# Moving the routing of the seventh batch into the last two groups of attention, and packing the eighth batch's steps closer

## The chip, the cores and the metric
The kernel runs on one core of a Trainium2 chip. The metric is the device time in microseconds (us) of the whole program. The engines are PE (TensorE, matrix products), DVE (VectorE), ACT (ScalarE), POOL (GpSimd) and SP (SyncE, which here only issues DMAs). Each engine works through its own list of instructions in order; semaphores tie the lists together, and an engine that waits holds back everything behind the wait in its own list.

## The reference
One transformer block with adaptive layer norm, 8 batches of 512 tokens, width 128, in float32:

```python
mod = (_silu(L0_c) @ L0_wmod).reshape(L0_c.shape[0], 6, 1, -1)
sa, ca, ga, sb, cb, gb = (mod[:, 0], mod[:, 1], mod[:, 2], mod[:, 3], mod[:, 4], mod[:, 5])
ga = (2 * (ga >= 0) - 1) * jnp.maximum(jnp.abs(ga), 0.25)
gb = (2 * (gb >= 0) - 1) * jnp.maximum(jnp.abs(gb), 0.25)
h = _layernorm(x, axis=-1) * (1 + ca) + sa
x = x + ga * _L0_attn_ref(h, L0_attn_Wq, L0_attn_Wk, L0_attn_Wv)
h = _layernorm(x, axis=-1) * (1 + cb) + sb
x = x + gb * _L0_ffn_ref(h, L0_ffn_router_w, L0_ffn_w1, L0_ffn_b1, L0_ffn_w2, L0_ffn_b2)
return x
```

The attention has 16 query heads of 8 and one shared key and value head. The feed-forward part is a mixture of 8 experts (128 to 512 to 128, exact GELU): a router gives each token 8 logits, the two largest are kept, and their experts' outputs are mixed by the softmax of the two logits.

## The kernel before, in words
The program has three stages. The first (`prepare_*`) normalises the input and computes queries, keys and values. The second is attention in 32 groups (`GROUPS`) of four heads: batch b has the groups 4b to 4b+3. The third is the expert stage: tokens have been scattered into rows sorted by expert (`h_sorted` in DRAM), and 78 tiles (`NTILES`) of 128 rows are worked through, 55 for the batches 0 to 5 (`TILES[0]`) and 23 for the batches 6 and 7. Batches are counted from 0, so the seventh is batch 6 (`LAST - 1`) and the eighth batch 7 (`LAST`).

**A group of attention.** For each of four blocks s of 128 keys, PE makes the scores of four heads in two halves u (`scores`, L957), ACT exponentiates each half (`exponentials`, L1134) and PE multiplies by the values (`values`, L967). Two groups ahead, PE makes the scores once more for the maxima (`maximum`, L926), which DVE takes (`take_maximum`, L1275); ACT copies the turned maxima (L1159), POOL splits them (`split`, L72 to L75) and SP moves them into the operands (`shift`, L819). So in the groups 30 and 31 there are no maxima left to take, and DVE has little to do. After a group, ACT copies its result out (`out_of_bank`, L1127) and SP moves the rows of its heads together by five DMAs (`regroup`, L829 and L830).

**Steps of a batch after its attention.** They are written into the loops by hand, a fixed number of groups after the batch: sums and heads are turned (PE L932 and L982, ACT copies L1150 and L1169), the attention is divided, gated and added (`add_attention`, L618, L620, L622), statistics (`stats`, L1291, on DVE), variance (L631 to L639), reciprocal root (`newton_root`, L647 to L652, always on POOL), normalised rows (`normalize_rows`, L1144, on ACT), `rows` (L661 to L665), rows turned (`turn_batch`, PE L1001, ACT copy L1173), router logits (PE L1009, ACT L1177), `top_two` (L688 to L700), `ranks` (PE L1018 and L1019, ACT L1183), `slots` (L720 to L727), and `route` (L734): two indirect DMAs of 128 rows each, for each of four blocks of tokens, so eight DMAs a batch, issued by POOL. For the batches 0 to 5 all of this lies in attention. For batch 6 the last part of it, and for batch 7 all of it, stands in the loop over tiles at fixed tile numbers (`if t == 8: turn_batch(LAST - 1)`), on each engine's list for itself.

**A tile t of the expert stage.** SP loads its rows (`load_tile`, L853). PE turns tile t+4 (`turn_rows`, L1026), makes the first product of tile t+2 (`up`, L1035) and the second of tile t (`down`, L1046). ACT applies GELU in four instructions (`gelu`, L1190). DVE copies the turned tile (`transposed`, L1307), its destination rows (L1311) and the expert's weights (`weights`, L1300), and adds the second bias (`results`, L1319). POOL scatters the result (`scatter`, L1469, one indirect DMA per tile). ACT runs up to two tiles ahead of DVE's `results`.

**Between the chunks.** When batches 0 to 5 are placed, DVE numbers the tiles (`count_tiles`, `number_tiles`), and SP writes filling rows behind each expert's rows (`fill`, L837, eight DMAs in two halves around the last `regroup`s). The same comes again for the batches 6 and 7: `fill(1, ...)` stands in SP's list between the loads of tile 54 and tile 55, and tile 55 can be loaded only when batches 6 and 7 are routed and filled.

**Order at the end of attention.** SP issues the loads of the tiles 0 to 7, then `regroup` of group 31 (L829 and L830, at `t == XD - 1`), then the load of tile 8. PE sets out on tile 0 when attention, weights and tile numbers are there.

## Time and profile before
| | |
|---|---|
| median of three runs | 681.05 us (680.46 to 684.31) |
| profiled execution | 677.33 us, of which the span from first to last instruction is 675.5 us |
| PE busy | 595.8 us (88%) |
| DVE busy | 497.0 us (74%) |
| ACT busy | 448.8 us (66%) |
| POOL busy | 356.6 us (53%) |
| DMA | 49.65 MB, mean 74 GB/s |

The durations below come from the one profiled execution, the median from three others. The prepare stage and attention take the first 470 us, the tiles from there to 656 us, and the last loads, mixing and stores the remaining 20 us. Busy shares are averages over stages with different limits, so the rows that count are those of the end of attention and of the expert stage. In a row of a timeline, the square brackets give the idle time of the engine just before it and the line that ended it; "remote" means that the profile found no instruction of an engine that ended it.

### The profile page before, as it was taken

The page shows a single profiled execution, that of the slowest core. Times are in us where ns is not written, and L with a number is a line of the kernel's source. Part 1 is how long each engine was busy: PE and PEld are TensorE (multiplying, and loading weights), DVE is VectorE, ACT ScalarE, POOL GpSimd, SP SyncE. Part 2 cuts the span into 40 slices and gives each one's busy share as a digit, 9 for nine tenths or more (in the row PEclk, how much of TensorE's full clock was granted, in tenths as well). Part 3 has the DMA queues.
Part 4 walks back from the last instruction along what each step waited for, and adds up shares of the span by engine and source line. Part 5 has one row for each costly group of instructions (what it writes and reads, how often), then busy time and mean ns, then how long its engine had stood idle before and what let it go on. Part 6 is the DMA issues. An engine that isn't in the chain of part 4 may idle for free.

```text
span 675.5 us, 19379 instructions
## 1 busy us (share of the span) xinstructions
PE 595.8 (88%) x6826; PEld 329.5 (49%) x6826; DVE 497.0 (74%) x1113; ACT 448.8 (66%) x795; POOL 356.6 (53%) x602
## 2 busy tenths in 40 slices
PE   2897999999999999999999999977997969779980
PEld 1342234433433433433433433422997969769980
DVE  5578999898887787798797797762565645555876
ACT  2473488888878778778778778658654534355771
POOL 5785101143465575675575675655454555645571
PEclk9897999999999999999999999979997998899995
DMA  7763500210300300301301300011221222224634
GB/s 214 272 180 101 148 8 12 75 27 9 93 16 23 102 18 22 102 16 31 95 15 31 95 15 24 20 50 45 70 72 43 68 54 69 64 68 128 200 100 148
DMA packets 46766, 49.65 MB, mean 74 GB/s; under 512 B 11168, under 2 KB 40912, under 8 KB 45936
## 3 DMA queue, kind: packets, MB, share of 16 engines
q1 hardware_dynamic: 38928, 37.20, 20.5%
q0 software_dynamic: 4544, 9.38, 4.2%
q10 hardware_dynamic: 3200, 1.84, 0.9%
q8 instruction: 57, 0.93, 0.6%
q14 instruction: 37, 0.30, 0.2%
HBM read 30.30 MB, written 17.47 MB: 71 GB/s over the span
## 4 chain that ended last, share of the span: by engine, by line
PE 64%; DVE 13%; issue 5%; POOL 5%; ACT 4%; SPq 4%; another core or an unknown queue 2%; DMA 2%; POOLq 0%; DVEq 0%; ACTq 0%
PE ps L926 14%; PE ps L967 14%; PE ps L957 12%; DVE neg_max L1275 11%; PE ps L1046 8%; PE ps L1035 7%; POOL P L258 4%; ACT P L1134 1%; ACT parts L1190 1%; PE ps L994 1%; PE ps L1009 1%; PE ps L945 1%; PE ps L1026 1%; SPq L829 1%
## 5 line engine op out<-in xcount | busy, mean ns | idle before, releaser
L1275 DVE TENSOR_REDUCE neg_max<-ps 128x1 f32<-128x512 f32 x512 | 320.0, 681 | 63.5 <-PE ps L926 55.4
L1134 ACT ACTIVATE P<-ps,zero 128x1024 f32<-128x1024 f32 x256 | 272.5, 1111 | 83.5 <-PE ps L957 79.2
L926 PE MATMUL ps<-K,Q 128*32 128x512 bf16 x2048 | 187.0, 386 | 7.1 <-DVE neg_max L1275 3.1
L957 PE MATMUL ps<-Q,K 128*32 128x512 bf16 x2048 | 156.7, 383 | 10.8 <-ACT P L1134 7.7
L967 PE MATMUL ps<-P,V 128*32 128x512 f32 x1024 | 134.8, 601 | 1.1 <-ACT P L1134 0.8
L1469 POOL DMA_INDIRECT y_rows<-P,to_now x78 | 78.8, 1010 | 83.9 <-DVE to_now L1311 36.4
L926 PEld LDWEIGHTS ps<-K,Q 128*32 128x32 bf16 x2048 | 54.0, 95 | 126.0 <-DVE neg_max L1275 75.8
L1190 ACT ACTIVATE parts<-ps,parts 128x128 f32<-128x128 f32 x252 | 70.5, 378 | 64.3 <-PE ps L1035 25.2
L957 PEld LDWEIGHTS ps<-Q,K 128*32 128x32 bf16 x2048 | 50.9, 97 | 78.8 <-issue 32.1
L1046 PE MATMUL ps<-W,parts 128*128 x504 | 72.2, 289 | 10.6 <-ACT parts L1190 9.6
L734 POOL DMA_INDIRECT h_sorted<-diag,slot x64 | 63.9, 998 | 28.3 <-POOL max_parts L75 13.3
L1035 PE MATMUL ps<-parts 128*128 128x128 f32 x504 | 71.0, 284 | 4.9 <-issue 3.9
L1046 PEld LDWEIGHTS ps<-W,parts 128*128 128x128 f32 x504 | 65.1, 202 | 12.1 <-issue 11.7
L1035 PEld LDWEIGHTS ps<-parts 128*128 128x128 f32 x504 | 64.5, 199 | 7.3 <-issue 5.7
L72 POOL CAST max_parts<-neg_max_T 16x128 bf16<-16x128 f32 x32 | 8.9, 279 | 111.7 <-ACT neg_max_T L1159 111.7
L1300 DVE COPY parts<-W 128x644 f32 x63 | 33.1, 525 | 19.8 <-issue 10.4
L1319 DVE TENSOR_TENSOR P<-ps,parts 128x128 f32<-128x128 f32 x63 | 17.8, 284 | 35.5 <-PE ps L1046 20.7
L967 PEld LDWEIGHTS ps<-P,V 128*32 128x32 f32 x1024 | 30.4, 110 | 20.9 <-issue 2.9
L258 POOL TENSOR_SCALAR P<-X,ln_mean,ln_rstd 128x128 f32<-128x128 f32 x28 | 26.3, 949 | 4.3 <-DVE ln_rstd L390 4.2
L1307 DVE COPY parts<-ps 128x128 f32<-128x128 f32 x63 | 17.8, 283 | 11.6 <-PE ps L1026 10.7
L1190 ACT ACTIVATE P<-ps,P 128x128 f32<-128x128 f32 x60 | 17.2, 380 | 11.0 <-PE ps L1035 6.2
L1026 PE MATMUL ps<-consts,xs 128*128 128x128 f32 x78 | 21.8, 284 | 0.9 <-DMA xs<-h_sorted 0.9
(203 smaller groups left out, 616.5 us busy)
## 6 DMA issues: line engine op xcount, KB each, us to landing
Q<-q_parts SPq DMA_DIRECT2D x24, 384.0 KB
xs<-h_sorted SPq DMA_DIRECT2D x78, 65.0 KB
W<-w_t SPq DMA_DIRECT2D x2, 2048.0 KB, 10.7
q_parts<-parts SPq DMA_DIRECT2D x8, 384.0 KB
Q<-y_rows SPq DMA_DIRECT2D x6, 512.0 KB
diag<-att_u SPq DMA_DIRECT2D x128, 16.0 KB
Q<-max_parts SPq DMA_DIRECT2D x96, 4.0 KB
out<-Q SPq DMA_DIRECT2D x6, 256.0 KB, 2.3
```

The source lines that it names most:

```text
L258: eng.tensor_scalar(xn[b % 2][:, t, :], X[:, n, :], ln_mean[:, n:n + 1], ln_rstd[:, n:n + 1], ALU.subtract, ALU.mult).then_inc(done, 1)
L734: eng.indirect_dma_start(h_sorted[chunk_of(b)], bass.IndirectOffsetOnAxis(ap=slot[p][:, k, t:t + 1], axis=0), hs[p][:, t, :], None).then_i ...
L926: ins = eng.matmul(ring_bank(*unit)[QUAD * q:QUAD * (q + 1), :], Q[buffer_of(g)][:, g % NG * G + j, at:at + QUAD], K[buffer_of(g)][:, 0, : ...
L957: ins = eng.matmul(bank(2 * u + j)[QUAD * q:QUAD * (q + 1), :], K[p][:, 1, at:at + QUAD], Q[p][:, g % NG * G + 2 * u + j, :], start=True, ...
L967: ins = eng.matmul(bank(7)[QUAD * j:QUAD * (j + 1), :], V[buffer_of(g)][:, s, :], P[s % 2][:, j, :], start=(s == 0), stop=(s == T - 1), ti ...
L1035: ins = eng.matmul(bank(t % UD)[:, TS * c:TS * (c + 1)], w1_now[t % HD][:, 128 * c:128 * (c + 1)], xsT[t % HD], start=True, stop=True)
L1046: ins = eng.matmul(bank(DOWN_BANK[t % 2])[:, 0:D], hid[t % HD][:, c, :], W2[:, bass.ds(e, 1), c, :].rearrange("p a d -> p (a d)"), start=( ...
L1134: nc.scalar.activation(P[s % 2][:, 2 * u:2 * u + 2, :], bank(2 * u, 2).rearrange("p (j t) -> p j t", j=2), ACT.Exp, bias=zero[:], scale=SC ...
L1190: nc.scalar.activation(hid[t % HD][:, c, :], bank(t % UD)[:, TS * c:TS * (c + 1)], ACT.Gelu, bias=w1_now[t % HD][:, F + c:F + c + 1]).then ...
L1275: eng.tensor_reduce(neg_max[g % 2][:, j * T + s:j * T + s + 1], ring_bank("maximum", g, s, j), AX.X, ALU.max, negate=True).then_inc(ring_u ...
L1300: eng.tensor_copy(w1_now[t % HD], W1[:, bass.ds(e, 1), :].rearrange("p a d -> p (a d)")).then_inc(w_copied, 1)
L1469: eng.indirect_dma_start(y_rows, bass.IndirectOffsetOnAxis(ap=to_now[t % YD][:], axis=0), ys[t % YD], None).then_inc(scattered[t % YD], 16)
```

## The change
All of batch 6's steps up to its slots leave the loop over tiles. In group 30 DVE adds the attention of batch 6, takes its statistics and variance ahead of `count_tiles` and `number_tiles`, and makes its `rows` after them. POOL's part is the reciprocal root alone, put between two routes of batch 5. ACT normalises the four blocks before the half (3, 0) of group 30. In group 31 PE turns the rows and makes the logits, ACT copies both, DVE ranks them (`top_two`); PE makes the ranks after its last values, ACT copies them before it loads the GELU table, and DVE makes the slots before its first `transposed`. POOL routes batch 6 after the scatters 1, 3, 5 and 7.

`regroup` of group 31 moves from SP's list to ACT's (`regroup_last`), before the first GELU. The steps of batch 7 are set to earlier tiles, in the same order and on the same engines as before; its `normalize_rows` is split over two tiles.

```diff
+        TURN_LATE, LOGITS_LATE = (GROUPS - 1, 0, 3), (GROUPS - 1, 1, 3)
...
                 for t in range(NTILES):
                     load_tile(t)
-                    if t == XD - 1:
-                        regroup(GROUPS - 1)
...
+                            if (g, s, j) == TURN_LATE:
+                                turn_batch(LAST - 1)
+                            if (g, s, j) == LOGITS_LATE:
+                                logits(LAST - 1)
...
                 values(GROUPS - 1, T - 1)
+                ranks(LAST - 1)
                 eng.wait_ge(experts_loaded, START + 4 * 16)
                 eng.wait_ge(ring_used, START + len(USED_AT))
-                eng.wait_ge(ring_copied, START + COPIED_AT["sums turned", LAST])
+                eng.wait_ge(ring_copied, START + COPIED_AT["ranks", LAST - 1])
...
+                    if t == 0:
+                        turn_sums(LAST)
                     if t == 2:
-                        turn_sums(LAST)
-                    if t == 5:
                         turn_heads(LAST)
-                    if t == 8:
-                        turn_batch(LAST - 1)
-                    if t == 11:
-                        logits(LAST - 1)
-                    if t == 19:
-                        ranks(LAST - 1)
-                    if t == 21:
+                    if t == 15:
                         turn_batch(LAST)
-                    if t == 24:
+                    if t == 17:
                         logits(LAST)
-                    if t == 32:
+                    if t == 22:
                         ranks(LAST)
...
+                def regroup_last():
+
+                    g = GROUPS - 1
+                    eng.wait_ge(att_out, START + g + 1)
+                    for j in range(G):
+                        at = ((NG - 1) * G + j) * DK
+                        eng.dma_start(heads_T[LAST % 2][at:at + DK, :], att_u[g % 2][QUAD * j:QUAD * j + DK, :]).then_inc(regrouped[g % 2], 16)
+                    eng.dma_start(sums_T[LAST % 2][(NG - 1) * G:, :], att_u[g % 2][DK:128:QUAD, :]).then_inc(regrouped[g % 2], 16)
...
+                            if (g, s, u) == (GROUPS - 2, 3, 0):
+                                normalize_rows(LAST - 1, range(T))
                 out_of_bank(GROUPS - 1)
+                ranks_out(LAST - 1)
                 nc.scalar.preload_act_table(ACT.Gelu)
+                regroup_last()
                 for t in range(NTILES):
                     gelu(t)
...
-                    if t == 16:
-                        normalize_rows(LAST, range(T))
...
+                    if t in (13, 14):
+                        normalize_rows(LAST, (2 * (t - 13), 2 * (t - 13) + 1))
...
                     if g == GROUPS - 2:
+                        eng.wait_ge(x1_own, START + (LAST - 1) * X1_OPS)
+                        add_attention(eng, LAST - 1)
+                        for t in range(T):
+                            stats(LAST - 1, t)
+                        variance(eng, LAST - 1)
                         count_tiles(eng, 0)
                         number_tiles(eng, 0)
+                        rows(eng, LAST - 1)
+                    if g == GROUPS - 1:
+                        top_two(Chain(eng, top_own, top_ops(LAST - 1)), LAST - 1)
...
+                slots(Chain(eng, slot_own, slot_ops(LAST - 1)), LAST - 1)
                 for t in range(TURNS):
                     transposed(t)
...
-                    if t in (12, 13):
-                        variance(eng, LAST, (t - 12,))
...
+                    if t in (9, 10):
+                        variance(eng, LAST, (t - 9,))
...
+                        newton_root(eng, LAST - 1)
                         route(eng, CHUNK[0] - 1, 3)
...
-                variance(eng, LAST - 1)
-                newton_root(eng, LAST - 1)
                 for t in range(NTILES):
                     scatter(t)
-                    if t == 4:
-                        rows(eng, LAST - 1)
-                    if t == 14:
+                    if t in (1, 3, 5, 7):
+                        route(eng, LAST - 1, (t - 1) // 2)
+                    if t == 10:
                         newton_root(eng, LAST)
-                    if t in (25, 27, 29, 31):
-                        route(eng, LAST - 1, (t - 25) // 2)
-                    if t in (38, 40, 42, 44):
-                        route(eng, LAST, (t - 38) // 2)
+                    if t in (26, 28, 30, 32):
+                        route(eng, LAST, (t - 26) // 2)
```

The first place is POOL's list in the expert stage, before. `y_rows` rows are scatters of tiles, `h_sorted` rows are routes (x2 is one call); the six rows from `root` on are the reciprocal root of batch 7.

```order
L1469 DMA y_rows<-P,to_now 10240x128 x5
L661 COPY diag<-consts 128x4
L663 TENSOR_TENSOR diag<-diag,mod_row 128x512
L665 TENSOR_TENSOR diag<-diag,mod_row 128x4x128
L1469 DMA y_rows<-P,to_now 10240x128 x10
L647 TENSOR_TENSOR root<-var,minus_half 128x4
L648 TENSOR_TENSOR newton<-var,root 128x4
L649 TENSOR_TENSOR newton<-newton,root 128x4
L650 TENSOR_SCALAR newton<-newton 128x4
L651 TENSOR_TENSOR rstd<-newton,root 128x4
L652 TENSOR_TENSOR shift<-less_mean,rstd 128x4
L1469 DMA y_rows<-P,to_now 10240x128 x11
```

The same place of the changed kernel, where the line numbers have grown by 6 (L1485 is `scatter`, L740 `route`, L653 the start of the root):

```order
L1485 DMA y_rows<-P,to_now 10240x128 x2
L740 DMA h_sorted<-diag,slot 10240x130 x2
L1485 DMA y_rows<-P,to_now 10240x128 x2
L740 DMA h_sorted<-diag,slot 10240x130 x2
L1485 DMA y_rows<-P,to_now 10240x128 x2
L740 DMA h_sorted<-diag,slot 10240x130 x2
L1485 DMA y_rows<-P,to_now 10240x128 x2
L740 DMA h_sorted<-diag,slot 10240x130 x2
L1485 DMA y_rows<-P,to_now 10240x128 x3
L653 TENSOR_TENSOR root<-var,minus_half 128x4
L654 TENSOR_TENSOR newton<-var,root 128x4
L655 TENSOR_TENSOR newton<-newton,root 128x4
```

Ahead of the reciprocal root of batch 7 stood 15 scatters and one `rows`; now there are 11 scatters and 8 routes.

The second place is ACT's list where attention ends and the tiles begin, before. L1134 is `exponentials`, L1127 `out_of_bank`, L1190 `gelu` (x4 a tile):

```order
L1134 ACTIVATE P<-ps,zero 128x1024 x7
L1127 COPY att_u<-ps 128x512
L1230 ACT_TABLE_LOAD
L1190 ACTIVATE parts<-ps,parts 128x128 x16
L1144 ACTIVATE diag<-X,shift,rstd 128x128 x4
```

The same place of the changed kernel (L1137 `exponentials`, L1130 `out_of_bank`, L1186 `ranks_out`, L1202 and L1203 `regroup_last`, L1193 `gelu`):

```order
L1137 ACTIVATE P<-ps,zero 128x1024 x3
L1130 COPY att_u<-ps 128x512
L1186 COPY rk<-ps 128x64
L1249 ACT_TABLE_LOAD
L1202 DMA diag<-att_u 8x512 x4
L1203 DMA sums_T<-att_u 4x512
L1193 ACTIVATE parts<-ps,parts 128x128 x12
```

Between the last copy out and the first GELU there are now a copy of the ranks and five DMA issues.

The third place is DVE's list at the same point, in the changed kernel (L1312 the last of the first four copies of weights, L726 to L733 `slots` of batch 6, L1319 the first `transposed`):

```order
L1312 COPY parts<-W 128x644
L726 TENSOR_TENSOR runs<-runs,rk 128x8 x4
L728 TENSOR_TENSOR slot_of<-rk,runs 128x32
L729 TENSOR_TENSOR slot_in<-hot,slot_of 128x64
L682 TENSOR_REDUCE slot_f<-slot_in 128x8
L732 COPY diag<-slot_f 128x4
L733 CAST slot<-slot_f 128x8
L1319 COPY parts<-ps 128x128
```

Before, L1307 (`transposed`) followed L1300 (`weights`) directly:

```order
L1300 COPY parts<-W 128x644
L1307 COPY parts<-ps 128x128
L1311 SCALAR_TENSOR_TENSOR to_now<-xs,own_slot 128x1
L1307 COPY parts<-ps 128x128
L1311 SCALAR_TENSOR_TENSOR to_now<-xs,own_slot 128x1
```

Nine instructions of DVE have come in front of the copy that PE's first product needs.

## Rows read from the trace of the kernel before

**Rows 1.** By stretch: PE, PEld, DVE, ACT, POOL busy; PE's granted clock, DMA share, GB/s

```profile
450.00:456.00 6.00, 6.00 (x48) 1.65 (x40) 0.51 (x3) 2.93 (x3) 4.09 (x6) 0.52 0.23 58
606.00:648.00 42.00, 41.26 (x368) 41.17 (x369) 31.52 (x104) 26.29 (x97) 23.69 (x24) 1.00 0.55 160
```

**Rows 2.** Stretches again, L1026 alone: the first x counts the tiles turned

```profile
500.00:516.00 16.00, 1.49 (x6) 0.72 (x5) 0.93 0.23 64
537.00:562.00 25.00, 2.51 (x8) 1.46 (x8) 0.86 0.23 62
575.00:607.00 32.00, 3.14 (x11) 1.66 (x11) 0.95 0.25 67
607.00:648.00 41.00, 5.79 (x22) 2.99 (x21) 1.00 0.55 161
```

**Rows 3.** Timeline of ACT, end of attention: start, duration, engine, line, count

```profile
458.04 3.12 ACT L1134 ACTIVATE P<-ps,zero 128x1024 f32<-128x1024 f32 x3 [0.53 <-remote]
...
470.33 0.58 ACT L1127 COPY att_u<-ps 128x512 f32<-128x512 f32 x1 [1.19 <-PE ps L967]
470.93 1.28 ACT L1230 ACT_TABLE_LOAD   x1
472.23 3.20 ACT L1190 ACTIVATE parts<-ps,parts 128x128 f32<-128x128 f32 x12
```

**Rows 4.** Timeline of SP's queue, same stretch

```profile
453.44 1.81 SPq L819 DMA_DIRECT2D Q<-max_parts  x3
...
475.24 3.04 SPq L829 DMA_DIRECT2D diag<-att_u  x4
478.32 0.53 SPq L830 DMA_DIRECT2D sums_T<-att_u  x1
```

**Rows 5.** Timeline of PE, end of attention and the tiles

```profile
470.19 0.44 PE L1026 MATMUL ps<-consts,xs 128*128 128x128 f32 x2
...
474.07 1.13 PE L1046 MATMUL ps<-W,parts 128*128 x8
...
480.25 0.39 PE L932 MATMUL ps<-consts,sums_T 16*128 16x16 f32 x4 [1.26 <-DMA sums_T<-att_u]
...
515.34 2.07 PE L1046 MATMUL ps<-W,parts 128*128 x8 [4.26 <-ACT parts L1190]
...
606.74 0.33 PE L1026 MATMUL ps<-consts,xs 128*128 128x128 f32 x1 [0.85 <-DMA xs<-h_sorted]
```

**Rows 6.** Timeline of POOL in the tiles

```profile
508.58 0.97 POOL L1469 DMA_INDIRECT y_rows<-P,to_now  x1 [1.28 <-DVE P L1319]
509.58 1.20 POOL L647 TENSOR_TENSOR root<-var,minus_half 128x4 f32<-128x4 f32 x1
...
538.25 0.96 POOL L734 DMA_INDIRECT h_sorted<-diag,slot  x1 [0.31 <-issue]
...
555.34 0.96 POOL L1469 DMA_INDIRECT y_rows<-P,to_now  x1 [2.45 <-DVE P L1319]
```

**Rows 7.** Timeline of ACT in the tiles

```profile
512.54 1.65 ACT L1144 ACTIVATE diag<-X,shift,rstd 128x128 f32<-128x128 f32 x4 [6.49 <-POOL shift L652]
...
583.96 1.14 ACT L1190 ACTIVATE parts<-ps,parts 128x128 f32<-128x128 f32 x4 [8.56 <-remote]
```

**Rows 8.** Timeline of DVE, group 30 and the tiles

```profile
443.84 0.19 DVE L744 CAST fill_at<-runs 1x8 int32<-1x8 f32 x1
...
494.86 0.68 DVE L620 TENSOR_TENSOR gated<-att,mod_row 128x512 f32<-128x512 f32 x1
...
506.09 0.16 DVE L639 TENSOR_TENSOR var<-var,newton 128x4 f32<-128x4 f32 x1
```

**Rows 9.** The chain that ended last, one piece: logits of batch 6

```profile
499.17 0.79 PE ps L1009 x8
```

**Rows 10.** Line L1018, and line L797: durations min/median/max in ns

```profile
L1018 PE MATMUL ps<-chosen,consts x16: 195/272/401, 185.2 to 556.8; 128*128 128x32 f32 x16
...
L797 ACTq DMA_DIRECT2D Q<-y_rows x4: 348/452/456, 663.0 to 664.4; - x4
```

77 lines of the change are left out of this document (35 added, 42 removed).

## The prediction
> **What bounds the kernel now.** I read the stretches first. From 606 to 648 us PE is busy 41.26 of 42 us and DVE 31.52, ACT 26.29, POOL 23.69 [rows 1]: an undisturbed tile is bound by PE alone, and 22 turned tiles in 41 us make 1.9 us a tile [rows 2]. Then I counted tiles in the stretches that fall short of that. The 6 tiles of 500 to 516 should take 11.4 us and take 16: 4.6 lost. The 8 of 537 to 562, where POOL routes batch 6, should take 15.2 and take 25: 9.8 lost. The 11 of 575 to 607, where it routes batch 7, should take 20.9 and take 32: 11.1 lost [rows 2]. So the expert stage loses time at a few places, and a change in it is worth what it does there.
>
> Next, the timelines of those places. At 512.54 ACT has waited 6.49 us for POOL's `shift`, the last of batch 7's root, and PE then waits 4.26 us for ACT and makes its next eight products in 2.07 us [rows 5, 7]. In the two routing stretches the waits are of another kind: ACT stands 8.56 us until 583.96 with "remote" as the cause, while POOL issues its indirect DMAs 1.26 us apart without a gap (0.96 and 0.30) [rows 6, 7]. The profile names no releaser; I take it as an effect of those trains of DMAs, since the stretch without routes, 607 to 648, has none of it. Last, the end of attention: there ACT is the engine that works without gaps (seven exponentials after the copy at 461), copies out at 470.33 and starts GELU at 472.23; PE turned the first tile at 470.19 [rows 3, 5].
>
> The span is 675.5 us, the profiled execution 677.33, the median of the three runs 681.05. I sum differences in the profiled execution and put them on the median.
>
> **End of attention: a loss.** ACT gets four normalised blocks (1.65 us for four, the row at 512.54) ahead of an exponential in front of which it was idle 0.53 us: +1.1 [rows 3, 7]. In group 31 it gets the copy of turned rows, as long as the copy of 128x512 at 470.33, 0.58, and the copy of logits, about 0.2: +0.8 [rows 3]. PE's additions there cost nothing, ACT hides them; if POOL's root came late, that cover would be gone (a rival below). DVE now does some 4.7 us (three operations at 0.68, four statistics, eight variance steps near 0.2) ahead of `count_tiles`, which started at 443.84 [rows 8]; SP's filling waits for that, and the `shift` of group 31 behind it in SP's list, issued at 453.44, moves to about 456.7 to 458.5 [rows 4]. It lands about 1.8 us later (as from 478.32 to 480.12, when PE could go on), near 460.4, just when the delayed ACT frees the banks. I count it as hidden, at up to +1.2.
>
> **Start of the tiles: a loss.** In front of PE's first turn now stand the ranks and ACT's copy of them: four matmuls near 0.27 each, overlapping, and 0.2, so +0.9 [rows 10]. Behind that, DVE makes nine chained instructions of slots (about 0.21 each, 1.9) before the copy that the first product needs. ACT, after the table load of 1.28, issues five DMAs before the first GELU. SP took 3.04 + 0.53 for the same five; ACT's own four issues at L797 took 0.45 each, so 2.3 at the least. I take 3.4, since it is the same transfer [rows 3, 4, 10]. First GELU: 472.23 + 1.9 + 0.2 + 3.4, less the small gaps, about 477.4. DVE's slots lie beside it. The second product of tile 0 was at 474.07 [rows 5] and comes to about 478.5: +4.4. Given back: PE no longer waits for the sums. It sat idle 1.26 until 480.25 (1.7 us over the period by the turns), because SP issued that regroup after eight tile loads, at 475.24 [rows 4, 5]. Issued by ACT at 474 to 477.4 it lands by 479.2, behind tile 0's second product. Net so far 4.4 − 1.7 and 0.4 for the turn of heads before I compare at tile 7, which both pay: **+3.1 us** for the end of attention and the start together, with +2 and +6 as ends.
>
> The Trainium skill ("DMA: Bandwidth & Descriptors", Issuing engines are not separate DMA queues) says that issuing from several engines only saves the time on the sequencer, usually small. Here the trace shows a wait of 1.26 us for a DMA that was late by its place in the list; by the page alone the move would be worth nothing, and the sum 1.7 us worse.
>
> **Work taken out of the tile loop: a gain.** PE bounds a tile, so each PE step of batch 6 that leaves it is time: turn of rows 0.4 (four like the sums' 0.39), logits 0.79 [rows 5, 9], ranks four at up to 0.27 with loads, about 0.7 [rows 10]. **−1.9 us.** The DVE and ACT steps of batch 6 were hidden and count nothing.
>
> **The wait for batch 7's root.** Before, DVE's variance was ready at 506.25 (0.16 from 506.09), but POOL first took scatter 14 from 508.58, began the root at 509.58 and needed 2.9 us [rows 6, 8]. Now the variance is at tile 10, the scatter ahead of the root is number 10, whose result DVE has before the variance, and ACT asks at tile 13: the same three tiles. If POOL is abreast, the root starts about 1 us after the variance instead of 3.3, ACT waits 4.2 instead of 6.49, and its first GELU comes after two blocks (0.82) instead of four (1.65). PE's idle 4.26 becomes about 1.2, and half of the slow 2.07 (against 1.13 at 474.07) goes with it. **−3.9 us**, ends −7 (no wait) and +3 (POOL behind by what it has more to do, below).
>
> **The routes.** Their number is the same, eight pairs. Batch 6's move from tiles 25 to 31 to tiles 1 to 7; batch 7's from 38 to 44 to 26 to 32. I take each stretch at what batch 6's cost, 9.8 less the ranks of batch 7 in it (0.9), 8.9; bounds 0 and 11.1, what the trace shows without and with [rows 2]. For batch 6 that is no change. For batch 7 it is 11.1 to 8.9, **−2.2 us**: filling, GELU and Exp tables and the load of tile 55 (PE idle 0.85 at 606.74) no longer fall into the same stretch [rows 5]. The filling still comes after the load of tile 54 in SP's list, but a chain of eight fills and one load is shorter than the nine tiles, 17 us, that PE has left.
>
> Sum: +3.1 − 1.9 − 3.9 − 2.2 = −4.9. On 677.33 that gives 672.4 for a profiled execution, on the median 676.2. I forecast 676 us.
>
> **Rivals.** (A) Slower: POOL's queue bounds the first fourteen tiles. Up to the root it has 11 scatters and 8 routes, 19 × 1.26 = 23.9 us, and PE needs 11 × 1.9 = 20.9. If the trains' stops do not let POOL catch up, it is 3.0 us behind, the gain at the root becomes a loss of 3.0, and the first stretch costs 11.1 instead of 8.9, as batch 7's did. Sum: 3.1 − 1.9 + 3.0 + 2.2 − 0.9 = +5.5, 686.6. It decides once POOL's lag at scatter 10 is over 2 us. For it: the row of 1.26 between issues. Against: in 537 to 562 POOL had the same mixture and was itself idle in it, 2.45 us before 555.34 [rows 6]. (B) About no change: the wait for the root merely moves with ACT's ask, as the distance of three tiles suggests; its −3.9 is 0: 680.1. (C) Clearly faster: the stops do not follow the routes, but what else lay in the old stretches. Then the early routes cost nothing and 8.9 more are gained: 667.3. For it: "remote" names no releaser. Against: the 8.56 us begin and end with the train.
>
> The Trainium skill speaks for C ("SBUF — State Buffer", Who interferes with whom): GpSimd shares a port pair with DVE alone, and PE and ACT never wait for anybody. By that rule routes could not stop ACT. The row of 8.56 us says that something did; the changed trace will say whether it moves with the routes.
>
> A late root in attention is part of A's side: POOL makes batch 6's root after two routes, ready near 456.6, and ACT asks at 457.5. One more us there is one us, and PE's clock, granted 0.52 from 450 to 456 after a pause, would fall again [rows 1].
>
> **Numbers.** Forecast 0.42, A 0.20, B 0.23, C 0.15. What can be told from no change is about 0.5%, 3.4 us: faster is under 677.6, slower over 684.5. Faster: most of the forecast and C, 0.52. Slower: A, 0.20. Same: B and the forecast's upper edge, 0.28. The forecast's own range is 672 to 680; with the others, 667 to 687 holds eight in ten.
>
> **What would show it.** In the changed trace: first turn near 473 and first GELU near 477; no PE wait at the sums; ACT's wait for the root at tile 13 near 4 us (over 8: A; over 6: B); "remote" stops of several us between tiles 1 and 9 and tiles 26 and 34 (none: C); no PE wait at tile 55. I am wrong in mechanism if group 30 or 31 grows by more than 3 us, or if the early stretch loses much more or less than 9 us.

## The result and the profile after

The changed kernel takes 683.99 us (median of 20 runs, 681.43 to 688.24), the kernel before in the same comparison 680.24 us. The ratio is 1.0058, interval [1.0037, 1.008]: slower by 0.6%, where faster was forecast. The profiled execution took 681.43 us (span 679.3), 4.1 us more than the 677.33 of the kernel before. The busy times hardly differ:

```profile
PE 595.3 (88%) x6826; PEld 327.9 (48%) x6826; DVE 501.4 (74%) x1127; ACT 450.1 (66%) x795; POOL 349.1 (51%) x588
```

The start of every turned tile on PE places the difference (L1030, L1026 before; the turn of tile 0 is at 470.19 before and at 475.20 after):

| stretch of turned tiles | before, us | after, us | difference | what moved |
|---|---|---|---|---|
| start of the program to 7 | 480.57 | 490.20 | +9.6 | end of attention, start of tiles |
| 7 to 20 | 26.87 | 36.70 | +9.8 | batch 6's routes and the wait for batch 7's root came, batch 6's turn and logits went |
| 20 to 32 | 32.02 | 24.68 | −7.3 | the wait for batch 7's root went |
| 32 to 45 | 35.69 | 36.25 | +0.6 | batch 7's routes in place of batch 6's |
| 45 to 54 | 28.58 | 17.74 | −10.8 | batch 7's routes went |
| 54 to 55 | 3.01 | 4.80 | +1.8 | wait for the load of tile 55 |
| 55 to 77 | 42.02 | 41.77 | −0.3 | nothing |

From tile 7 on the change gains 6.2 us, where the prediction's terms add up to 8.0. The start costs 9.6, where it said 3.1: 2.0 of them stand at the first scores of group 31 (461.26 against 459.30), 3.0 more come until the turn of tile 0, and 4.6 between the turns of the tiles 0 and 7.

An undisturbed tile takes 1.90 us, so what a stretch takes beyond that is what it lost. Read so, after the change the tiles 8 to 18 lost 8.7 us (batch 6's routes) and the tiles 19 and 20 lost 3.35 (the root). Before, the root cost 7.24, at the tiles 22 and 23. The stretch 32 to 45 lost 11.0 us before (batch 6's routes) and 11.6 after (batch 7's); 45 to 54 lost 11.5 before (batch 7's) and 0.6 after.

**The start.** The answer to [rows 4], SP (SPq: the issuing of a DMA, its length, the line):

```profile
450.10 4.67 SPq L843 DMA_DIRECT2D h_sorted<-fill_rows  x4
454.81 2.84 SPq L835 DMA_DIRECT2D diag<-att_u  x4
457.69 0.53 SPq L836 DMA_DIRECT2D sums_T<-att_u  x1
458.26 1.81 SPq L825 DMA_DIRECT2D Q<-max_parts  x3
```

The `shift` of group 31 goes out at 458.26, 4.8 us later than the 453.44 of before, since the first filling waits for `count_tiles` and the shift stands behind both the filling and a regroup. PE waits for it, then ACT for PE (the third row is before's, the first scores of group 31 there):

```profile
461.26 1.04 PE L961 MATMUL ps<-Q,K 128*32 128x512 bf16 x8 [5.15 <-DMA Q<-max_parts]
```
```profile
462.42 1.11 ACT L1137 ACTIVATE P<-ps,zero 128x1024 f32<-128x1024 f32 x1 [4.26 <-PE ps L961]
```
```profile
459.30 0.62 PE L957 MATMUL ps<-Q,K 128*32 128x512 bf16 x8 [0.27 <-ACT P L1134]
```

In the changed kernel PE had ended all that stands in front of these scores at 456.11, 3.2 us sooner than the kernel before started them. So group 30 had brought a gain, and the wait turned it into a loss of 2.0.

Then DVE's list between attention and the first tile:

```profile
470.76 0.42 DVE L694 TENSOR_TENSOR diag<-lg 128x256 f32<-128x256 f32 x1 [12.08 <-ACT lg L1180]
...
473.81 0.18 DVE L706 TENSOR_SCALAR chosen<-rank 128x32 f32<-128x32 f32 x1
475.03 0.50 DVE L1312 COPY parts<-W 128x644 f32 x1 [1.04 <-issue]
...
477.27 0.50 DVE L1312 COPY parts<-W 128x644 f32 x1 [0.24 <-issue]
...
479.42 0.17 DVE L733 CAST slot<-slot_f 128x8 int32<-128x8 f32 x1
479.63 0.29 DVE L1319 COPY parts<-ps 128x128 f32<-128x128 f32 x1
```

`top_two` waits 12.08 us for the logits, and behind it stand the weights of the first four tiles (L1312). Before, DVE had copied them during attention, by 464.5; now they run from 475, one after another, then the slots, and only at 479.63 the copy of the first turned tile (L1319). PE had turned that tile at 475.20 and stood, and went on at half its clock. First the stretches (length, busy time of PE, its weight loads, DVE, ACT and POOL, granted clock of PE, share and rate of the DMAs), then PE's first product, then ACT:

```profile
475.00:480.00 5.00, 0.62 (x6) 0.38 (x5) 3.92 (x16) 1.90 (x3) 0.00 (x0) 0.97 0.30 71
480.00:483.00 3.00, 2.94 (x14) 2.97 (x15) 0.79 (x5) 0.85 (x4) 0.00 (x0) 0.50 0.16 39
```
```profile
480.06 2.04 PE L1039 MATMUL ps<-parts 128*128 128x128 f32 x8 [4.44 <-DVE parts L1319]
```
```profile
475.49 1.25 ACTq L1202 DMA_DIRECT2D diag<-att_u  x1
475.64 1.28 ACT L1249 ACT_TABLE_LOAD   x1
476.77 1.99 ACTq L1202 DMA_DIRECT2D diag<-att_u  x3
478.79 0.54 ACTq L1203 DMA_DIRECT2D sums_T<-att_u  x1
482.14 1.14 ACT L1193 ACTIVATE parts<-ps,parts 128x128 f32<-128x128 f32 x4 [5.23 <-PE ps L1039]
```

PE was busy 0.62 us in five, and then had 0.50 of its clock, that is 1.2 GHz, from 480 to 483: 2.04 us for a product that takes 1.06 later. ACT's five issues took 3.8 us (3.4 were priced) and were over at 479.33, before the first product: they weren't what the first GELU waited for. The first GELU is at 482.14, not near 477.

**The routes** (L740), among the scatters (L1485), at tiles 1 to 7, and ACT's GELU (L1193) beside them:

```profile
500.07 1.01 POOL L1485 DMA_INDIRECT y_rows<-P,to_now  x1 [0.30 <-issue]
501.39 0.96 POOL L1485 DMA_INDIRECT y_rows<-P,to_now  x1 [0.31 <-issue]
502.65 0.96 POOL L740 DMA_INDIRECT h_sorted<-diag,slot  x1 [0.30 <-issue]
503.92 1.07 POOL L740 DMA_INDIRECT h_sorted<-diag,slot  x1 [0.30 <-issue]
505.29 0.96 POOL L1485 DMA_INDIRECT y_rows<-P,to_now  x1 [0.30 <-issue]
```
```profile
507.62 1.14 ACT L1193 ACTIVATE P<-ps,P 128x128 f32<-128x128 f32 x4 [8.00 <-remote]
...
562.62 3.21 ACT L1193 ACTIVATE parts<-ps,parts 128x128 f32<-128x128 f32 x12 [8.57 <-remote]
```

The stops moved with the routes. Before, they ended at 583.96 (8.56 us, [rows 7]) and here:

```profile
554.39 1.14 ACT L1190 ACTIVATE parts<-ps,parts 128x128 f32<-128x128 f32 x4 [6.42 <-remote]
```

DVE stands too (3.48 us until 507.65), and PE after it.

**The root and tile 55.** The wait for POOL's `shift` is 3.07 us (6.49 in [rows 7]); the load of tile 55 is late, as before:

```profile
520.37 0.88 ACT L1147 ACTIVATE diag<-X,shift,rstd 128x128 f32<-128x128 f32 x2 [3.07 <-POOL shift L658]
```
```profile
610.37 0.33 PE L1030 MATMUL ps<-consts,xs 128*128 128x128 f32 x1 [2.74 <-DMA xs<-h_sorted]
```

### The profile page after: what moved, and what is told of

The parts are those of the page before. It is cut to its first block, busy times and chain, and to the rows that moved or that the text cites. A ratio compares the mean times of both kernels' runs of the same rounds, so it can differ in the third digit from the quotient of the medians.

```text
span 679.3 us, 19382 instructions
## 1 busy us (share of the span) xinstructions
PE 595.3 (88%) x6826; PEld 327.9 (48%) x6826; DVE 501.4 (74%) x1127; ACT 450.1 (66%) x795; POOL 349.1 (51%) x588
## 4 chain that ended last, share of the span: by engine, by line
PE 63%; DVE 15%; POOL 6%; issue 5%; SPq 3%; ACT 2%; DMA 2%; another core or an unknown queue 2%; DVEq 1%; POOLq 0%; ACTq 0%
PE ps L930 15%; PE ps L971 14%; PE ps L961 12%; DVE neg_max L1287 10%; PE ps L1050 8%; PE ps L1039 7%; POOL P L258 4%; PE ps L998 1%; PE ps L1013 1%; PE ps L949 1%; PE ps L1030 1%; SPq L843 1%; PE ps L1005 1%; ACT parts L1193 1%
## 5 line engine op out<-in xcount | busy, mean ns | idle before, releaser
L1137 ACT ACTIVATE P<-ps,zero 128x1024 f32<-128x1024 f32 x256 | 272.8, 1112 | 84.5 <-PE ps L961 82.2
L1485 POOL DMA_INDIRECT y_rows<-P,to_now x78 | 79.0, 1013 | 98.7 <-DVE to_now L1323 61.4
L1193 ACT ACTIVATE parts<-ps,parts 128x128 f32<-128x128 f32 x252 | 71.0, 380 | 63.1 <-PE ps L1039 30.4
L740 POOL DMA_INDIRECT h_sorted<-diag,slot x64 | 64.6, 1009 | 28.6 <-POOL max_parts L75 13.4
L1050 PE MATMUL ps<-W,parts 128*128 x504 | 69.0, 280 | 3.6 <-ACT parts L1193 1.4
L1050 PEld LDWEIGHTS ps<-W,parts 128*128 128x128 f32 x504 | 62.5, 195 | 4.7 <-issue 4.4
L1312 DVE COPY parts<-W 128x644 f32 x63 | 32.8, 520 | 19.1 <-issue 9.5
L1193 ACT ACTIVATE P<-ps,P 128x128 f32<-128x128 f32 x60 | 17.2, 373 | 16.8 <-remote 8.0
L1030 PE MATMUL ps<-consts,xs 128*128 128x128 f32 x78 | 21.5, 280 | 3.2 <-DMA xs<-h_sorted 2.7
L1319 DVE COPY parts<-ps 128x128 f32<-128x128 f32 x63 | 17.9, 284 | 8.1 <-issue 4.1
```

What stands on the lines that cost most here:

```text
L740: eng.indirect_dma_start(h_sorted[chunk_of(b)], bass.IndirectOffsetOnAxis(ap=slot[p][:, k, t:t + 1], axis=0), hs[p][:, t, :], None).then_i ...
L1050: ins = eng.matmul(bank(DOWN_BANK[t % 2])[:, 0:D], hid[t % HD][:, c, :], W2[:, bass.ds(e, 1), c, :].rearrange("p a d -> p (a d)"), start=( ...
L1137: nc.scalar.activation(P[s % 2][:, 2 * u:2 * u + 2, :], bank(2 * u, 2).rearrange("p (j t) -> p j t", j=2), ACT.Exp, bias=zero[:], scale=SC ...
L1193: nc.scalar.activation(hid[t % HD][:, c, :], bank(t % UD)[:, TS * c:TS * (c + 1)], ACT.Gelu, bias=w1_now[t % HD][:, F + c:F + c + 1]).then ...
L1312: eng.tensor_copy(w1_now[t % HD], W1[:, bass.ds(e, 1), :].rearrange("p a d -> p (a d)")).then_inc(w_copied, 1)
L1485: eng.indirect_dma_start(y_rows, bass.IndirectOffsetOnAxis(ap=to_now[t % YD][:], axis=0), ys[t % YD], None).then_inc(scattered[t % YD], 16)
```

## Experiments

All ratios are to the kernel before, run on the same chip beside it; the square brackets hold the 95% interval. The changed kernel stands at 1.0058 [1.0037, 1.008], and differences to it are of ratios (1% is 6.8 us). The same point of the program comes at different times in different traces (group 30 starts between 442.9 and 447.3 us in the comparisons with stops), so traces are compared by lengths of stretches and by waits.

**1. The shift first.** In SP's list the filling goes behind the regroup and the shift of group 31:

```diff
-                    if g == GROUPS - 2:
-                        fill(0, range(E // 2))
                     if g > 0 and g + 1 < GROUPS:
                         regroup(g - 1)
                     if g + 1 < GROUPS:
                         shift(g + 1)
+                    if g == GROUPS - 2:
+                        fill(0, range(E // 2))
```

> The changed kernel, but SP issues the regroup of group 29 and the shift of group 31 ahead of the first half of the filling. Theory 1 (start order): PE's 5.15 us wait for the shift in front of group 31 goes, ACT's 4.26 us with it; attention ends 3.5 to 4.5 us earlier and the whole is 3 to 4.5 us below the changed kernel, 680 us against its 684. Rival (ACT's DMA issues and the early routes are what costs): the shift's wait is given back at the start of the tiles, under 1.5 us gained.

0.9985 [0.9961, 1.0008]: 5.0 us below the changed kernel. The waits of PE and ACT for the shift are gone. The turn of tile 0 is at 471.54; that of tile 1, at 472.48, waits 0.63 us for its load. The kernel before was not run in this order; there PE waited 0.27 us in front of these scores, and for ACT.

**2. The weights first.** `for t in range(AHEAD): weights(t)` with its two waits moves in front of `top_two(..., LAST - 1)`.

> The changed kernel, but DVE copies the weights of the tiles 0 to 3 before it ranks batch 6 (top_two) in group 31. Theory 1: the copies (475.0 to 477.8) leave the chain logits, top_two, weights, slots, first turned copy; PE's 4.44 us wait in front of the first product shrinks by 2.7 to 3 us, the whole by 2 to 3. Rival: ACT's first GELU cannot come before its DMA issues end at 479.3 (table load and five issues), so PE's wait only moves to the second product and less than 1 us is gained.

1.003 [1.0011, 1.0049]: 1.9 us less. The interval overlaps that of the changed kernel, so the total alone doesn't prove it; the trace does: PE waits 2.49 us for DVE in place of 4.44.

**3. Both, and the slots behind the first transposed tiles.**

```diff
-                slots(Chain(eng, slot_own, slot_ops(LAST - 1)), LAST - 1)
                 for t in range(TURNS):
                     transposed(t)
+                slots(Chain(eng, slot_own, slot_ops(LAST - 1)), LAST - 1)
```

> The changed kernel with the shift first, the weights first, and the slots of batch 6 after the first four turned copies. Theory 1: gains of 4, 2.8 and 1.5 us add up to 7 to 8, since each was on the path; 676 to 677 us. Then the change would be faster than the kernel before by 3 to 4 us. Rival: behind the first two, ACT's first GELU at the end of its five DMA issues is the bound; the sum stops at 4 to 5 us.

0.9941 [0.9918, 0.9965]: 8.0 us below the changed kernel, and faster than before. So the order of two lists, SP's and DVE's, was worth more than the start's excess over its forecast, 6.5 us. From the first scores of group 30 to the turn of tile 7 it takes 39.42 us here, 47.33 in the changed kernel and 37.73 before. Not all of it is waits taken away: group 30, to the first scores of group 31, takes 12.99 us here against 16.45 before, a gain that the prediction doesn't have. There ACT stood 3.34 us ("remote") until 446.98 in the kernel before, and 1.92 us until 445.59 in the changed one; what made the difference isn't shown. Now ACT's issues do end last:

```profile
477.13 0.54 ACTq L1203 DMA_DIRECT2D sums_T<-att_u  x1
477.72 2.18 ACT L1193 ACTIVATE parts<-ps,parts 128x128 f32<-128x128 f32 x8 [2.44 <-PE ps L1039]
```

**4. Those issues back on SP**, behind the load of tile 3 (`if t == 3: regroup(GROUPS - 1)`), the rest as in 3.

> The changed kernel with the three edits at the start (shift of group 31 ahead of the first filling, first weights ahead of top two, slots behind the first four transposed tiles), and the last head rows moved back from ACT's queue to SP's, behind the load of tile 3. Theory (with the three edits the first GELU starts as soon as ACT's five issues are out, so these 3.8 us are now what bounds the start, partly covered by PE's cold first products): the first GELU starts 1 to 3 us earlier, and the whole is 1 to 2 us below the version with the issues on ACT, which was 8.0 us below the changed kernel. Rival (the sums then land late, as before the change): PE waits 1 to 2 us at the sums and the whole is the same as, or above, the version with ACT's issues.

0.9996 [0.9975, 1.0018]: 3.7 us worse than 3. The first GELU came at 473.54, 4.2 us earlier, as the theory had it; but PE then waited for a third thing, the load of tile 4, which stood behind five more issues:

```profile
469.11 3.73 SPq L859 DMA_DIRECT2D xs<-h_sorted  x4
472.88 2.75 SPq L835 DMA_DIRECT2D diag<-att_u  x4
475.67 0.53 SPq L836 DMA_DIRECT2D sums_T<-att_u  x1
477.49 1.48 SPq L859 DMA_DIRECT2D xs<-h_sorted  x2
```
```profile
479.43 0.47 PE L1032 MATMUL ps<-consts,xs 128*128 128x128 f32 x1 [3.89 <-DMA xs<-h_sorted]
```

So ACT's queue is the better place, at least against this one; the old place, behind the load of tile 7, was not run with the three edits.

**5. Routes one at a time, spread.** Batch 6's eight DMAs behind the scatters 1, 4, ..., 22, batch 7's behind 26, 28, ..., 40.

> The changed kernel, but the routes of the batches 6 and 7 go out as single indirect DMAs: batch 6 after the scatters 1, 4, ... 22, batch 7 after the scatters 26, 28, ... 40, so that POOL has a pause after three or four DMAs. Theory 2 (trains): engines stop only when POOL issues about four or more indirect DMAs without a pause; ACT's stops of 8.00 and 8.58 us go, and the whole is 8 to 15 us below the changed kernel for batch 6's part alone. Rival (number): each route DMA costs its 1 to 1.5 us of the others wherever it stands, 16 of them as before; no change within 2 us.

0.9991 [0.9973, 1.0008]: 4.6 us less than the changed kernel, under what was expected. No stop of 8 us is left, but several of 3 to 6, beside trains of three to five DMAs, and tile 55 no longer waits (1.90 us after tile 54).

**6. A train without routes.** Scatters 62 to 66 are held and sent with that of 67:

```diff
-                    scatter(t)
+                    if not 62 <= t < 67:
+                        if t == 67:
+                            eng.wait_ge(y_out, START + 68)
+                            for held in range(62, 67):
+                                scatter(held)
+                        scatter(t)
```

> The changed kernel, in which POOL holds back the scatters of tiles 62 to 66 and issues them with that of tile 67 in one train of six. There are no routes anywhere near. The 16 buffers of results cover the delay, so no engine waits for a scatter by the program's semaphores. Train theory (what stops ACT is any train of back-to-back indirect DMAs on POOL, and routes are no different from scatters): ACT, which has 2.4 us or less of idle beside each train of three there, has one stop of 6 to 8 us beside the train of six (about 7.6 us at 1.26 us each), PE then one of 2 to 4 us, and the whole is 2 to 5 us above the changed kernel; where the trains of three stood between tiles 62 and 67 ACT's stops are gone. Rival (routes are special: they write sorted rows that the loads wait for, or the 128-row gather of X is what blocks): no ACT stop over 3 us at the train of six, the whole within 1 us of the changed kernel.

1.0151 [1.0101, 1.0201]: 6.3 us more than the changed kernel. The turns of tiles 76 and 77 took 5.34 and 3.93 us, where each takes 1.90. So the routes as such aren't needed for a stop: plain scatters of POOL end to end make one too.

**7 to 9. The train at tiles 56 to 61, without and with pauses.** The same hold for tiles 56 to 60: once as it is, once with three chained memsets of 16 columns behind each scatter from there on (each waits for the one before), once with a single memset that no DMA waits for. Each was run twice, with one trace.

```diff
+                def pause():
+                    for _ in range(3):
+                        eng.memset(apart[:], 0.0).then_inc(paused, 1)
+                        pauses.append(1)
+                        eng.wait_ge(paused, START + len(pauses))
```

> The twin: the changed kernel, in which POOL holds the scatters of tiles 56 to 60 and sends them with that of tile 61 in one train, without pauses. The same kind of train at tiles 62 to 67 cost PE 5.5 us in its own turns and the whole 6 us. Train theory: ACT and then DVE stop 2.5 to 8 us from about 2 us after the train's begin, PE loses 4 to 6 us within three tiles of it, and the whole is 4 to 7 us above the changed kernel. Rival (the stop came from the place near the end of the program, where the combining loads run too): under 2 us lost here.

> The changed kernel, in which POOL holds the scatters of tiles 56 to 60, sends them with that of tile 61, and puts three small chained memsets (16 columns) behind each of them and behind every later scatter. So POOL still issues six and more indirect DMAs on end, but with a pause between any two. It is to be read beside its twin without memsets. Theory A (only DMAs with 0.30 us between them stop ACT; a pause of some tenths of a us lets ACT go on): no stop of ACT over 3 us and turns of PE every 1.9 us from tile 66 to 77, where the twin shows stops of 2.5 us and more and 5 us lost; the end may be later by POOL's backlog. Theory B (each indirect DMA costs the others a fixed time, pauses or not, and what counts is their number in a stretch): ACT's and PE's losses are the same in both.

> The twin kernel with the train of six (scatters of tiles 56 to 60 held and sent with that of 61), now with a single memset of 16 columns, not waited for, behind each of them and each later scatter: spacing about 1.4 us, where it was 1.26 without and about 2.15 with three chained ones. Theory A1 (any other instruction of POOL between two indirect DMAs ends the train for the others): no ACT stop over 2 us and PE's turns stay at 1.90 us, as with the three memsets. Theory A2 (what counts is how long POOL pauses between DMAs): with 0.45 us in place of 0.30 the stops stay, PE loses 5 to 8 us in three tiles, as in the twin without memsets.

Without pauses, ratio 1.0149 [1.0083, 1.0215]: POOL's train, then ACT and DVE, which stand under it:

```profile
635.12 0.96 POOL L1485 DMA_INDIRECT y_rows<-P,to_now  x1 [0.30 <-issue]
636.39 1.23 POOL L1485 DMA_INDIRECT y_rows<-P,to_now  x1 [0.31 <-issue]
...
641.71 0.96 POOL L1485 DMA_INDIRECT y_rows<-P,to_now  x1 [0.30 <-issue]
```
```profile
639.57 0.62 ACT L1193 ACTIVATE parts<-ps,parts 128x128 f32<-128x128 f32 x2 [4.26 <-remote]
643.98 2.17 ACT L1193 ACTIVATE parts<-ps,parts 128x128 f32<-128x128 f32 x8 [2.12 <-remote]
```
```profile
643.86 0.29 DVE L1331 TENSOR_TENSOR P<-ps,parts 128x128 f32<-128x128 f32 x1 [7.08 <-remote]
```

PE's turns of tiles 70 and 71 took 7.67 and 3.62 us. With the three memsets (L1485 here, scatter L1493) the gap is 1.08 us and more:

```profile
638.07 0.96 POOL L1493 DMA_INDIRECT y_rows<-P,to_now  x1 [0.62 <-POOL apart L1485]
639.04 0.46 POOL L1485 MEMSET apart<- 128x16 f32 x3
640.12 1.00 POOL L1493 DMA_INDIRECT y_rows<-P,to_now  x1 [0.62 <-POOL apart L1485]
```

and every turn from tile 62 to 77 takes 1.89 or 1.90 us, with ACT idle at most 0.76 us between two tiles, though POOL issues just as many DMAs. The total (1.0321 [1.0252, 1.0389]) is longer because POOL's backlog now ends last. With a single memset the spacing stayed at 1.27 us, since 0.14 us fits into the gap; ACT stood 4.40 and 2.21 us, DVE 7.33, and the ratio was 1.0157 [1.0105, 1.0208]. So in these traces theory A holds for pauses near a microsecond and not for very short ones.

**10. The single memset behind every DMA of the tiles**, in the changed kernel, the kernel before, and the version of experiment 12.

> The changed kernel with a single memset, not waited for, behind every indirect DMA of the tiles, between the two of a pair too; order and places of all else as they are. By A1 the stops at the two stretches of routes go and the whole is 12 to 18 us below the changed kernel, about 667 to 672 us. By A2: the same time to 3 us more.

> The kernel before with the same memsets. By A1 it gains as much as the changed kernel does, 12 to 18 us, and what is left between the two is the start alone: about 8 to 10 us for the start, less 2 us of PE work, less the shorter wait for the root (3 us), so before is still 2 to 5 us the faster of the two. By A2: the same time to 3 us more.

> The version with five edits (14 us below the changed kernel) with a single memset, not waited for, behind every scatter and route of the tiles. By A1 the stops of ACT that are left there (5.7, 5.5 and several near 3 us) go, PE's losses at tiles 19, 27, 36 and 44 with them, and the whole is 6 to 10 us less, near 661 to 664 us. By A2 nothing changes but POOL's 0.15 us for each of 94 DMAs: the same time to 2 us more.

1.0066 [1.0037, 1.0095], 0.9999 [0.9978, 1.002] and 0.9864 [0.983, 0.9897], where the same kernels without memsets have 1.0058, 1 and 0.9851: nothing, as A2 has it.

**11. Batch 7's steps at their old tile numbers**, batch 6 moved.

> The changed kernel with one part undone: all steps of batch 7 on PE, ACT, DVE and POOL stand at the tile numbers of the kernel before (sums at tile 2, root at 14, normalising at 16, logits at 24, routes at 38 to 44). Batch 6 stays in attention and its routes at tiles 1 to 7. Theory: closer steps moved batch 7's routes and took the load wait of tile 55 away or left it; the stretch of routes costs the same wherever it stands (8 to 11 us), and the wait for the root shrank because the stretch around it has no scatter between variance and root. So the time is within 2 us of the changed kernel, with ACT's stops of 8 us at tiles 38 to 44 in place of tiles 26 to 32, ACT's wait for the root near 3 us, and the load of tile 55 late by 1 to 3 us more, since fills and routes fall together. Rival 1 (closer steps were the gain of the change): 4 to 6 us slower than the changed kernel, with a root wait of 6 us again. Rival 2 (closer steps were part of the loss): 3 us or more faster than the changed kernel.

1.0098 [1.0065, 1.013]: 2.7 us more than the changed kernel, with intervals that overlap. The wait for the root is 6.16 us again, not the 3 us expected, so rival 1 was right in kind: with closer steps that wait is half as long, 3.07.

**12. Five edits together**: the three of experiment 3, the spread of 5, and `fill(1, (t - 45,))` behind each of the loads 45 to 52 in place of all eight between two loads. Then the same with batch 7's routes wider apart (26, 29, 31, 34, 36, 39, 41, 44).

> The changed kernel with five edits: the shift of group 31 ahead of the first filling in SP's list; DVE's first weights ahead of batch 6's top two; DVE's slots of batch 6 behind the first four transposed tiles; route DMAs one at a time, each between two scatters; and the second filling split into eight parts, one behind each of the loads 45 to 52. Theory (the start's order costs 8 us, long trains 4.5 us, the filling beside them 2 to 3 us, and the three add): 14 to 15 us below the changed kernel, about 668 to 671 us where the kernel before is 681. Rival (the gains overlap, since the spread routes begin where the start's waits still gave ACT a lead): 10 us or less below the changed kernel, 673 us or more. Second rival for the filling: its parts delay each tile load behind them, and PE waits at tiles 53 to 61 instead of at 55 alone; then 11 to 13 us.

> The version with all five edits (three at the start, single spread routes, split filling: 14 us below the changed kernel), with batch 7's eight routes wider apart: behind scatters 26, 29, 31, 34, 36, 39, 41 and 44 in place of 26, 28, ..., 40. There PE still lost 3.6 us at tile 36 and 3.8 us at tile 44. Theory (length of trains): one route per 2.5 scatters needs 4.4 us of POOL in 4.7 us, so the trains get shorter, and these losses shrink to about half: 2 to 4 us less than the five edits together. Rival (the losses are due to scatters that come in bursts, whatever the distance of routes, or the last route at scatter 44 now delays the load of tile 55): the same time within 1.5 us, or up to 3 us more with a wait for the load of tile 55.

669.70 us, ratio 0.9851 [0.9814, 0.9889]: 14.1 us below the changed kernel, and the lowest ratio of all versions. 8.0 of experiment 3 and 4.6 of experiment 5 make 12.6. The other 1.5 would be the filling's, but no run has it alone, and it is within the noise. The turn of tile 55 follows in 1.90 us, as it did in experiment 5 without the split filling. Spread wider: 0.9887 [0.9844, 0.993], no better.

**13. The kernel before with single routes and the split filling.**

> The kernel before (batch 6 still routed inside the tiles), with two of the later edits: route DMAs one at a time, each behind its own scatter, batch 6's at tiles 25 to 32 and batch 7's at 38 to 45, and the second filling one expert behind each of the loads 45 to 52. Between the slots of a batch and the first load that needs its rows there are only eight scatters here, so the spread is one route per scatter, where the changed kernel has room for one route per three or two scatters. Theory (what counts is how long POOL issues indirect DMAs without a pause; one route per scatter every 1.9 us needs 2.5 us of POOL, so it still makes trains): the stretches of the routes still lose 6 to 10 us each, the filling gives 1 to 2 us, and the whole is 0 to 3 us below the kernel before; so the room that the early batch 6 leaves is what makes the spread pay. Rival (single routes are enough, wherever they stand): 6 us or more below the kernel before, and moving batch 6 was not needed for it.

1.0017 [0.9988, 1.0046]: nothing. With eight scatters between slots and load there is no room to spread, and the stops stay (6.32 us for the turn of tile 47). So moving batch 6 is what gives the room, and the change as made didn't use it. Other spacings in the kernel before were not run.

**14. Longer pauses.** A single memset that the next scatter waits for, in the train at 56 to 61; and the version of 12 with three chained memsets behind each single route.

> The twin with the held train of six (tiles 56 to 60 with 61), with one memset of 16 columns behind each scatter that the next one waits for: by the row of three (0.15 us each, and 0.62 us until the next DMA starts) the gap is about 0.75 us and the spacing 1.7 to 1.8 us, between 1.27 (stops: ACT 4.4 and 2.2, DVE 7.3, PE loses 7 to 8 us) and 2.15 us (no stop). If the waiting of POOL for itself ends a train, or a gap of 0.75 us is enough: PE's turns stay at 1.90 us from 62 to 77. If it takes a full pause of about 1 us: PE loses 3 us or more.

> The version with five edits, batch 7's routes at scatters 26, 29, 32, 35, 38, 41, 44 and 46, and three chained memsets (POOL's gap 1.08 us) behind each single route. Four indirect DMAs and one pause need 5.8 us of POOL in three tiles, 5.7 us of PE and more with batch 7's steps, so POOL is just abreast. Theory (stops grow with the length of a train without pause): trains are cut to three or four, ACT's stops to 2 to 3 us which its lead covers, and the whole is 2 to 6 us below the version with five edits, 664 to 668 us. Rival (POOL, now full, falls behind: the root of batch 7 comes later, scatters run in longer trains to catch up, and the last routes delay the load of tile 55): the same time or up to 5 us more than the version with five edits.

Here the kernel before itself took 647.73 us (17 runs, all between 646.08 and 651.52), against 678.8 to 683.4 in the other comparisons, and neither trace has one "remote" wait of ACT of 2 us or more, not even beside four DMAs end to end:

```profile
536.88 0.96 POOL L1494 DMA_INDIRECT y_rows<-P,to_now  x1 [0.62 <-POOL apart L1486]
538.15 1.03 POOL L1494 DMA_INDIRECT y_rows<-P,to_now  x1 [0.31 <-issue]
539.49 0.96 POOL L1494 DMA_INDIRECT y_rows<-P,to_now  x1 [0.30 <-issue]
540.75 1.05 POOL L742 DMA_INDIRECT h_sorted<-diag,slot  x1 [0.30 <-issue]
```
```profile
541.93 1.14 ACT L1195 ACTIVATE P<-ps,P 128x128 f32<-128x128 f32 x4 [0.76 <-PE ps L1041]
543.83 1.14 ACT L1195 ACTIVATE parts<-ps,parts 128x128 f32<-128x128 f32 x4 [0.76 <-PE ps L1041]
545.72 1.14 ACT L1195 ACTIVATE parts<-ps,parts 128x128 f32<-128x128 f32 x4 [0.76 <-PE ps L1041]
```

The first, 663.36 us, has the ratio 1.0227 [1.0182, 1.0273]. Neither run can tell what a pause does. But the kernel before was about 32 us, 5%, faster here than elsewhere. That would be the worth of its stops, attention included (from 200 to 400 us PE did 2752 instructions in the trace of the second, 2668 in before's), if nothing else differed; it has no trace of its own here, so this isn't shown. The ratio of the second is 1.0031 [1.0008, 1.0053], and its losses are where POOL is full: ACT waits 5.83 us for the root, and PE 3.28 us for the load of tile 55.

The first run holds one more answer, since up to tile 55 its kernel is the changed kernel as it is. The tiles 8 to 18 lost nothing there, but ACT waited longest for the root:

```profile
504.90 0.96 POOL L1493 DMA_INDIRECT y_rows<-P,to_now  x1 [0.30 <-issue]
506.16 0.96 POOL L1493 DMA_INDIRECT y_rows<-P,to_now  x1 [0.30 <-issue]
507.14 1.05 POOL L654 TENSOR_TENSOR root<-var,minus_half 128x4 f32<-128x4 f32 x1
```
```profile
509.62 0.88 ACT L1148 ACTIVATE diag<-X,shift,rstd 128x128 f32<-128x128 f32 x2 [6.96 <-POOL shift L659]
```

The variance was ready at 501.83. POOL, with its DMAs end to end from 484.02, came to the root 5.3 us later. That is rival A: POOL's queue bounds the first tiles, once the stops no longer give it time to catch up.

## Why the prediction was wrong

**The failed step: the end of attention and the start, +3.1, measured +9.6.** Two things in it. The `shift` of group 31 was counted as hidden, up to +1.2, with its issue between 456.7 and 458.5. It went out at 458.26, inside that range, but the scores that need it were not held back until 460.4 by anything else, as the prediction had it: PE had ended its other work at 456.11, and waited 5.15 us. Putting the shift first gave 5.0 us back. And of DVE only the nine instructions of the slots were counted, beside ACT's issues. That `top_two`, which waits for the logits until 470.76, stands in front of four weight copies was overlooked: the note that a wait holds back what is behind it was applied to SP and ACT, not to DVE. Those copies and the slots, moved (experiment 3 against 1), were another 3.0 us. These 8.0 us are more than the 6.5 that were missing; against them stands that group 30 became shorter than before (experiment 3), which no term has. With 6.5 us more at the start the forecast would have been 682.5.

**The terms that held.** The root: by the turns it cost 7.24 us before and 3.35 after, a gain of 3.9, as said; ACT's wait fell from 6.49 to 3.07 us (to 4.2, it was said), and experiment 11 gives 2.7 us for the closer steps altogether. But it held by the stops: in experiment 14, where nothing stopped, the same steps waited 6.96 us. PE steps of batch 6: the three tiles that held them before (13, 16 and 24) lost 2.0 us together, where 1.9 were said. Routes of batch 6: 8.7 us lost where 8.9 were said. ACT's five issues: 3.8 us (3.4 said). No PE wait at the sums: right. ACT's root of batch 6 in attention: in time, the four blocks at 455.52 without a wait.

**A term that did not hold.** Batch 7's routes were to cost 8.9 for 11.1, because filling and tile 55 would no longer meet them. They cost as much as before: 11.6 us in the stretch 32 to 45, where 11.5 had been lost from 45 to 54. And tile 55 waits 2.74 us, where none was said: the eight fills take 5.30 and 4.55 us with a gap, and the load goes out at 608.42. By the turns, routes and tile 55 together gave about nothing in place of −2.2. With spread routes alone (experiment 5) tile 55 didn't wait.

**The sums.** The +3.1 holds 0.4 for the turn of heads, which both kernels pay, so it belongs in no difference. The −0.9 in rival A's sum comes from no row.

**The rivals.** A (POOL's queue makes the root late): its sign came true and not its mechanism, since the root's first instruction started 1.1 us after the variance was ready; that the total rose was no merit of it. Its mechanism came with the run without stops, where it was 5.3 us. B (the root's wait merely moves): no, 3.07. C (stops don't follow the routes): no. They followed, and a train of plain scatters makes them as well.

The Trainium skill ("SBUF — State Buffer", Who interferes with whom) has PE and ACT wait for nobody when GpSimd works. ACT's 8.00 us beside POOL's train, the 4.26 us beside the train of scatters alone and their absence with pauses do not fit that rule, taken as one on whole engines; the port may well be blameless, since no run here shows by what path the train holds ACT. That stays open, as does why one comparison in six had no stops at all: its chip carries the same number as that of experiments 7, 8, 13 and the second part of 12, where there were stops.

Whether the change is faster or slower than before where nothing stops wasn't measured. An estimate: the first trace of experiment 14 spans 661.0 us, of which 5.3 are the longer end behind its last turn (32.5 us, 27.1 in the changed kernel), so the changed kernel would span about 656 us, against about 646 for the kernel before beside it. So the change would cost more there, not less.

## What to carry to other kernels

When a step that waits is put into an engine's list, write down all that stands behind it there, for every engine that gets such a step, and ask of each item when it was done before; an idle engine's cheap copies are the easiest to overlook. A DMA's place in a list is worth its wait: a shift of 1.8 us of issue, 4.8 us late, cost 5.0. And look at how densely POOL issues indirect DMAs: three in a row went with a stop of 2.8 us, eight with one of 8.0, in engines that have nothing to do with them. So early steps paid here only when the room that they give was used to spread them. Last, a wait that a stop hides comes back when the stop goes: the root's was 3.07 us with stops and 6.96 without.

## What was not expected of the hardware

While POOL issues indirect DMAs 1.26 us apart, ACT stands (8.0 and 8.6 us beside trains of eight and seven in the changed kernel, 2.8 beside one of three), then DVE (3.5 to 7.3), then PE. Beside the long trains of routes they went on 1.4 to 1.5 us after the last DMA ended; beside the train of plain scatters ACT went on once in its midst. At a spacing of 2.1 us nothing stopped, in the one trace that has it. Between the two is not measured, since the one run there fell where nothing stopped. The effect isn't always there: in one comparison of six it was absent from both traces, and the kernel before was about 32 us faster.
